# Rotary products on GpSimd in two halves of 128 tokens, and three moves in the instruction orders of GpSimd and ScalarE

## The chip, the cores and the metric

One Trainium2 chip, one core. The time is the device time of one execution in microseconds; three executions were timed, and one more was profiled. A core has a matrix engine (TensorE, PE in the profile), VectorE (DVE), ScalarE (ACT), GpSimd (POOL) and SyncE (SP), whose queue issues nearly all transfers here. Each engine works through its own instruction list in order, and they meet only in semaphores.

## The reference

One layer of a vision transformer on 32 images of 3x224x224: patch embedding, causal attention with rotary positions, and a feed-forward part with fake quantisation. The change lies in the rotary part.

```
h = patches(x) @ W.T + b                     # 32 images x 256 tokens x 256
a = layernorm(h)
q = rope((a @ wq) as 16 heads x 16)          # rope: [t1*cos - t2*sin, t1*sin + t2*cos]
k = rope((a @ wk) as 4 heads x 16); v = a @ wv
attn = softmax(causal(q k^T / 4)); h = h + (attn v) @ wo
f = fake_quant(layernorm(h))                 # one scale over the whole tensor
h = h + fake_quant(silu(f @ Wg.T) * (f @ Wu.T)) @ Wd.T    # weights quantised by row
```

## The kernel before, in words

The first part of the kernel is a software pipeline over images, one step for each. The second part is the feed-forward part, which begins when all images have passed, because its scale is a maximum over all of them. The change touches the first part alone.

In step x each engine runs a list written out by hand, the function `step` in its block, over several images at once. PE embeds image x+3 (`patch`), projects x+2 to q, k and v (`project`, token block tb = 0 or 1 of 128 tokens each), makes the scores of x+1 from which a bound of each row's maximum is taken (`unit_pair`, six of them, "units"), the scores of x-1 and x proper (`score_pair`, eight of them, all in one pair of PSUM banks), the product with the values (`attend`, two halves), the transposes of the result (`o_turn`) and the output projection of x-2 (`out_project`). ScalarE takes the exponential of each score pair (`exp_pair`, L829), takes q, k, v out of PSUM (`projected`, L791, one for each token block), copies v (`values`, L798), writes the high half-precision parts of q and k into two stacks (`high`, L807 and L809, for the units; `fill_stack`, L820 to L822, for the scores), converts the next input (`x_high`, L781) and the attention result (`on_high`, L844), takes out the attention product (`o_copy`, L837) and the embedding (`embedded`, L767 and L772). GpSimd multiplies and adds for the rotation (`rotate_cross` L997, `rotate` L986, `add_rotated` L1011), clears the triangle of each exponential (`mask`, L978), and makes the low part of the input (`x_low`, L1017) and two small powers (L1024). VectorE reduces the units (`reduce_pair`, L1205), writes low parts (`low`, L1191 and L1193; `h_low`, L1211; `on_low`, L1270), normalises the attention product (`o_normalise`, L1252), adds the residual (`residual`, L1262) and does the statistics. SP turns the stacks by DMA transposes in a fixed order in each step: the normalised embedding (L380), the attention result (`turn_on`, L410), the unit stack (`turn_max`, L388), the score stack (`turn_stack`, L400).

The links that the text below follows: `score_pair` i waits for the exponential i-1, since it writes the same banks. `attend` half 0 waits for mask 3, half 1 for mask 7. The rotation waits for `projected`; `high` and `fill_stack` wait for the sum `qk`; `low` waits for `fill_stack`. `on_high` waits for `o_normalise`, `on_low` for `on_high`, `turn_on` for `on_low`, `out_project` for `turn_on`, `residual` for `out_project`. The instructions of VectorE stand in this order: reduce 0, reduce 1, reduce 2, `h_low`, reduce 3, `o_normalise`, reduce 4, `on_low`, reduce 5, `low`, `residual`, and then reduce 0 of the next step, with small statistics between. A unit waits for the reduce of the unit before it.

Of the kernel before, what the change touches and what calls it, by code (L numbers as in the profile page):

```python
# [103 lines left out]
def wait(eng, sem, value):  # L104

    if isinstance(value, int) and value <= 0:
        return
    eng.wait_ge(sem, value)
# [12 lines left out]
def vit_layer(nc, x_t, w_emb, w_qkv, w_o, w_gate, w_up, w_down, clips, rope, eye, tri, out):  # L121
    with ExitStack() as ctx:
# [639 lines left out]
        def _(act):  # L762
# [20 lines left out]
            def projected(x, tb):  # L783
                z = x + 2
                act.wait_ge(done["qkv"], z.n * 2 + (tb + 1))
                if tb == 0:
                    act.wait_ge(rstd_ready, z.n + 1)
                    wait(act, rot_a_ready, z.n)
                    wait(act, rot_b_ready, z.n)
                    wait(act, v_ready, z.n)  # L790
                act.activation(qkv[:, tb, :], shared[JOBS.index(("qkv", tb)) % 2][:, 0:QKV_COLS],  # L791
                               ACT.Copy, scale=rstd[:, tb:tb + 1]).then_inc(read["qkv"], 1)
# [9 lines left out]
            def high(x):  # L802

                z = x + 2
                act.wait_ge(qk_ready, z.n + 1)
                wait(act, max_turned[z.parity - 1], (z + -1).half * 16 + 16)
                act.activation(max_stack[:, :, 0:HEADS, 0:16], qk[:, :, 0:HEADS, :], ACT.Copy, scale=MAX_SCALE)  # L807
                for odd in range(2):
                    op = act.activation(max_stack[:, :, HEADS + 5 * odd:HEADS + 3 + 5 * odd:2, 0:16],  # L809
                                        qk[:, :, HEADS + odd:QK:2, :], ACT.Copy, scale=MAX_SCALE)  # L810
                op.then_inc(high_ready, 1)

            def fill_stack(x):

                z = x + 2
                stack = stacks[z.parity]
                act.wait_ge(qk_ready, z.n + 1)
                wait(act, first_turned[z.parity], z.half * 32)
                wait(act, second_turned[z.parity], z.half * 32)
                act.activation(stack[:, :, :, 16:32], qk[:, :, :, :], ACT.Copy)  # L820
                act.activation(stack[:, :, 0:HEADS, 0:16], qk[:, :, 0:HEADS, :], ACT.Copy)
                act.activation(stack[:, :, HEADS:QK, 32:48], qk[:, :, HEADS:QK, :], ACT.Copy).then_inc(stack_filled, 1)  # L822
# [50 lines left out]
            def step(x):  # L873
                early, late = x + 1, x + -1
                if (x + -1).exists():
                    exp_pair(late, 0)
                if (x + -2).exists():
                    o_copy(late + -1, 1)
                if x.exists():
                    values(late)  # L880
                if (x + -1).exists():
                    exp_pair(late, 1)
                if (x + 1).exists():
                    projected(late, 0)
                    projected(late, 1)
                if (x + -1).exists():
                    exp_pair(late, 2)
                    exp_pair(late, 3)
                if (x + 4).exists():
                    x_high(early)  # L890
                if (x + -2).exists():
                    on_high(late)
                if (x + -1).exists():
                    exp_pair(late, 4)
                if (x + 1).exists():
                    high(late)
                if (x + -1).exists():
                    exp_pair(late, 5)
                if (x + 1).exists():
                    fill_stack(late)  # L900
                if (x + 3).exists():
                    embedded(early)
                if (x + -1).exists():
                    exp_pair(late, 6)
                    o_copy(late, 0)
                    exp_pair(late, 7)
                if (x + -3).exists():
                    normalise2(x)
                if x.known and x.n == -2:
                    weights_turned_copy()  # L910
# [61 lines left out]
        def _(pool):  # L972
# [5 lines left out]
                pool.affine_select(out=p, in_=p, pattern=[[0, 4], [1, P]], compare_op=ALU.is_ge,  # L978
                                   fill=0.0, base=0, channel_multiplier=-1).then_inc(masked, 1)

            def rotate(x):

                z = x + 2
                pool.wait_ge(read["qkv"], z.n * 2 + 2)
                wait(pool, qk_ready, z.n)
                pool.tensor_tensor(rot_a, qk_of_qkv, rope_s[:, 0].to_broadcast([P, TB, QK, HD]),  # L986
                                   ALU.mult).then_inc(rot_a_ready, 1)

            def rotate_cross(x):

                z = x + 2
                pool.wait_ge(read["qkv"], z.n * 2 + 2)
                wait(pool, qk_ready, z.n)
                for half in range(2):
                    to = slice(8 * half, 8 * half + 8)
                    of = slice(8 - 8 * half, 16 - 8 * half)
                    op = pool.tensor_tensor(rot_b[:, :, :, to], qk_of_qkv[:, :, :, of],  # L997
                                            rope_s[:, 1, :, :, to].to_broadcast([P, TB, QK, 8]), ALU.mult)
                op.then_inc(rot_b_ready, 1)

            def flat(t):
                return t.rearrange("p b h d -> p (b h d)")

            def add_rotated(x):
                z = x + 2
                wait(pool, high_ready, z.n)
                wait(pool, stack_filled, z.n)
                wait(pool, low_ready, z.n)
                pool.wait_ge(rot_b_ready, z.n + 1)
                pool.wait_ge(rot_a_ready, z.n + 1)  # L1010
                pool.tensor_tensor(flat(qk), flat(rot_a), flat(rot_b), ALU.add).then_inc(qk_ready, 1)  # L1011

            def x_low(v):
                if v.known and v.n == 0:
# [12 lines left out]

            def step(x):
                early, late = x + 1, x + -1
                if (x + -1).exists():  # L1030
                    mask(late, 1)
                if (x + 1).exists():
                    rotate_cross(late)
                    rotate(late)
                    add_rotated(late)
                if (x + -1).exists():
                    mask(late, 2)
                    mask(late, 3)
                    mask(late, 4)
                if (x + 4).exists():  # L1040
                    x_low(early + 3)
                if (x + -1).exists():
                    mask(late, 5)
                    mask(late, 6)
                    mask(late, 7)
                if x.exists():
                    mask(x, 0)
                if (x + 2).exists():
                    power(var_ready, (x + 2).n, rstd, var, rstd_ready, read["qkv"])
                if (x + -2).exists():  # L1050
                    power(var2_ready, (late + -1).n, rstd2s, var2, rstd2_ready, xn2_ready)
# [452 lines left out]
```

## Time and profile before

| | us |
|---|---|
| median of three executions | 823.68 |
| the three | 821.96, 823.68, 827.12 |
| the profiled execution, its time | 827.79 |
| its span from first to last instruction | 826.0 |

| engine | busy us | share of the span |
|---|---|---|
| PE | 669.9 | 81% |
| DVE | 669.2 | 81% |
| ACT | 591.2 | 72% |
| POOL | 571.7 | 69% |

The image pipeline fills most of the span, at about 18 us for a step; the feed-forward part takes the rest. The mean granted TensorE clock is 0.947 of full speed, and 1.00 in the steps that are looked at below. Busy shares are means over all that, so they don't say what a step waits for; for that one step is laid out engine by engine.

### The profile page before, as it was taken

To read this page: it belongs to the slowest core of one execution; us is meant where nothing else is said; L and a number is where in the kernel's file an instruction comes from. 1 tells how busy PE (TensorE), PEld (TensorE's weight loads), DVE (VectorE), ACT (ScalarE), POOL (GpSimd) and SP (SyncE) were. 2 spreads that over 40 slices of the span, in tenths; PEclk is the share of its full clock that TensorE was granted. 3 is DMA by queue.
4 is the path that set the end of the run, shared out by engine and by line. 5 is a ranking of instruction groups with operands and counts; after the bars stand their busy time and mean duration, and the time that the engine had idled before them with its cause. 6 is when DMAs were issued, how large, how long until landed. Compare 5 with 4: busy or idle time off the path is not lost. (4 is left out here: it accounts for less than half of the span.)

```text
span 826.0 us, 20673 instructions
## 1 busy us (share of the span) xinstructions
PE 669.9 (81%) x6706; PEld 384.2 (47%) x6706; DVE 669.2 (81%) x1052; ACT 591.2 (72%) x972; POOL 571.7 (69%) x561
## 2 busy tenths in 40 slices
PE   3577888888888888898888888889766459997894
PEld 2354555454555555555555555555332223332663
DVE  5954889888988898988889889898663359999894
ACT  4345778787788777778877877887665258886783
POOL 0455778787888788888878888886553148884363
PEclk9687999999999999999999999999897769999798
DMA  8235667667566666556656655665443112221499
GB/s 278 58 72 111 129 122 145 144 131 123 127 144 141 134 150 143 126 122 147 144 133 153 140 126 126 144 143 114 92 78 73 50 38 52 51 43 21 68 175 165
DMA packets 245383, 96.56 MB, mean 117 GB/s; under 512 B 222432, under 2 KB 240608, under 8 KB 245344
## 3 DMA queue, kind: packets, MB, share of 16 engines
q1 hardware_dynamic: 236896, 87.69, 48.7%
q0 software_dynamic: 8448, 8.39, 7.0%
q8 instruction: 20, 0.33, 0.2%
q14 instruction: 19, 0.16, 0.1%
HBM read 24.74 MB, written 16.78 MB: 50 GB/s over the span
## 5 line engine op out<-in xcount | busy, mean ns | idle before, releaser
L1205 DVE TENSOR_REDUCE act_all<-pair 128x4 f16<-128x1024 f32 (+1 forms) x192 | 234.4, 1221 | 21.6 <-PE pair L535 20.9
L978 POOL TENSOR_SCALAR_AFFINE_SELECT act_all<-act_all 128x512 f32<-128x512 f32 x128 | 104.5, 827 | 72.5 <-ACT act_all L829 72.5
L829 ACT ACTIVATE ffn<-pair 128x768 f32<-128x768 f32 x128 | 103.2, 806 | 67.3 <-PE pair L552 67.0
L484 PE MATMUL pair<-act_all 128*128 128x256 f16 (+1 forms) x960 | 118.2, 277 | 21.8 <-DVE act_all L1252 18.5
L978 POOL TENSOR_SCALAR_AFFINE_SELECT ffn<-ffn 128x512 f32<-128x512 f32 x128 | 94.0, 736 | 57.8 <-ACT ffn L829 57.0
L829 ACT ACTIVATE act_all<-pair 128x768 f32<-128x768 f32 x128 | 104.1, 813 | 30.7 <-PE pair L552 28.2
L484 PEld LDWEIGHTS pair<-act_all 128*128 128x128 f16 (+1 forms) x960 | 90.8, 99 | 41.5 <-issue 23.3
L1017 POOL TENSOR_TENSOR act_all<-act_all 128x1280 f16<-128x1280 f32 x31 | 81.7, 2636 | 18.3 <-ACT act_all L781 18.3
L550 PE MATMUL pair<-act_all 64*128 64x256 f16 x512 | 73.2, 282 | 18.9 <-DMA act_all<-act_all 10.9
L1191 DVE TENSOR_TENSOR act_all<-act_all 128x512 f16<-128x512 f32 x32 | 40.9, 1279 | 49.1 <-ACT act_all L822 49.1
L498 PE MATMUL pair<-act_all 128*128 128x384 f16 x384 | 76.4, 337 | 0.2 <-ACT act_all L767 0.2
L939 ACT ACTIVATE ffn<-pair,gate_scale 128x512 f32<-128x512 f32 x96 | 60.9, 654 | 15.5 <-PE pair L710 8.0
L591 PE MATMUL pair<-act_all 128*128 128x256 f16 x384 | 51.0, 286 | 17.9 <-DMA act_all<-ffn 17.7
L1270 DVE TENSOR_TENSOR ffn<-act_all,ffn 128x512 f16<-128x512 f32 x32 | 54.4, 1701 | 11.6 <-ACT ffn L844 11.5
L997 POOL TENSOR_TENSOR act_all<-act_all 128x320 f32<-128x320 f32 x64 | 54.5, 871 | 13.3 <-ACT act_all L791 13.3
L837 ACT ACTIVATE act_all<-pair 128x512 f32<-128x512 f32 x64 | 38.0, 593 | 34.0 <-PE pair L570 34.0
L550 PEld LDWEIGHTS pair<-act_all 64*128 64x128 f16 x512 | 25.1, 93 | 76.7 <-issue 36.2
L522 PE MATMUL pair<-act_all 64*128 64x256 f16 x512 | 50.1, 274 | 13.2 <-DVE act_all L1205 12.3
L535 PE MATMUL pair<-act_all,eye_wide 64*128 64x128 bf16 (+1 forms) x768 | 60.5, 236 | 0.0
L1024 POOL TENSOR_TENSOR act_all<-act_all 128x2 f32<-128x2 f32 x64 | 43.9, 701 | 22.4 <-DVE act_all L1290 14.1
L552 PE MATMUL pair<-act_all 64*128 64x128 f16 x512 | 57.5, 220 | 0.0
L1077 POOL TENSOR_TENSOR act_all<-ffn 128x512 f32<-128x512 f32 x32 | 40.8, 1274 | 21.2 <-ACT ffn L927 21.2
(135 smaller groups left out, 1517.8 us busy)
## 6 DMA issues: line engine op xcount, KB each, us to landing
act_all<-x_t SPq DMA_DIRECT2D x32, 640.0 KB, 4.2
out<-act_all SPq DMA_DIRECT2D x32, 256.0 KB, 2.6
out<-ffn POOLq DMA_DIRECT2D x16, 512.0 KB, 6.9
act_all<-act_all SPq DMA_TRANSPOSE x192, 3.0
act_all<-w_down SPq DMA_DIRECT2D x1, 704.0 KB, 8.6
act_all<-w_emb SPq DMA_DIRECT2D x1, 640.0 KB, 4.0
ffn<-w_gate SPq DMA_DIRECT2D x1, 640.0 KB, 7.0
ffn<-w_up SPq DMA_DIRECT2D x1, 640.0 KB, 7.4
```

Source lines behind the costliest of these rows:

```text
L484: mm = pe.matmul(b, xs[0:k, sx, c, tb * P:(tb + 1) * P], we[0:k, sw, c, :], start=(c == 0 and (sx, sw) == PARTS[0]), stop=(c == KC - 1 and ...
L498: mm = pe.matmul(b[:, 0:QKV_COLS], h_t[:, sx, tb, c, :], wqkv[:, sw, c, :], start=(c == 0 and (sx, sw) == PARTS[0]), stop=(c == DC - 1 and ...
L535: mm = pe.matmul(on_diagonal, eye_wide[rows, at_:at_ + P], tri_b[rows, rows].rearrange("p (a t) -> p a t", a=1).to_broadcast([64, n_, 64]) ...
L550: pe.matmul(b[:, 0:TOKENS], op[rows, k, 0:P], op[rows, pair_, :], start=True, stop=True)
L552: mm = pe.matmul(b[:, TOKENS:3 * P], op[rows, k, P:TOKENS], op[rows, pair_, P:TOKENS], start=True, stop=True)
L829: act.activation(probs[i // 4][:, o:o + 2, 0:3, :].rearrange("p h k s -> p h (k s)"), pair[1][:, :].rearrange("p (h c) -> p h c", h=2)[:, ...
L939: act.activation(silu[m % 3][:, 0:cols], bank[2 + m % 3][:, 0:cols], ACT.Silu, scale=gate_scale[:, m:m + 1]).then_inc(silu_ready, 1)
L978: pool.affine_select(out=p, in_=p, pattern=[[0, 4], [1, P]], compare_op=ALU.is_ge, fill=0.0, base=0, channel_multiplier=-1).then_inc(maske ...
L997: op = pool.tensor_tensor(rot_b[:, :, :, to], qk_of_qkv[:, :, :, of], rope_s[:, 1, :, :, to].to_broadcast([P, TB, QK, 8]), ALU.mult)
L1017: pool.tensor_tensor(x_parts[v.parity][:, 1], xt[v.parity], x_parts[v.parity][:, 0], ALU.subtract).then_inc(x_low_ready, 1)
L1205: dve.tensor_reduce(to, pair[2][:, :].rearrange("p (k g t) -> p k g t", k=2, g=n_), AX.X, ALU.max).then_inc(unit_reduced, 1)
L1270: dve.tensor_tensor(on_parts[:, 1], on.rearrange("p b e -> p (b e)"), on_parts[:, 0], ALU.subtract).then_inc(on_low_ready, 1)
```

## The change

GpSimd's rotation is split by token block. `rotate(x, tb)` does the two cross products and then the straight product of one block of 128 tokens, and `add_rotated(x, tb)` its sum; before, each instruction covered both blocks. The first block's products now wait only for that block's `projected`. Both blocks are placed ahead of mask 1 instead of behind it. On ScalarE, `projected` of block 0 moves ahead of exponential 1 (block 1 stays behind it), `high` moves ahead of exponential 4, and `fill_stack` ahead of exponential 5. `high` and `fill_stack` still wait for both blocks. The semaphores' counts follow: two for each image where there was one.

```diff
--- before.py
+++ after.py
@@ -783,10 +783,10 @@
             def projected(x, tb):
                 z = x + 2
                 act.wait_ge(done["qkv"], z.n * 2 + (tb + 1))
+                wait(act, rot_a_ready, z.n * 2 + (tb - 1))
+                wait(act, rot_b_ready, z.n * 2 + (tb - 1))
                 if tb == 0:
                     act.wait_ge(rstd_ready, z.n + 1)
-                    wait(act, rot_a_ready, z.n)
-                    wait(act, rot_b_ready, z.n)
                     wait(act, v_ready, z.n)
                 act.activation(qkv[:, tb, :], shared[JOBS.index(("qkv", tb)) % 2][:, 0:QKV_COLS],
                                ACT.Copy, scale=rstd[:, tb:tb + 1]).then_inc(read["qkv"], 1)
@@ -802,7 +802,7 @@
             def high(x):
 
                 z = x + 2
-                act.wait_ge(qk_ready, z.n + 1)
+                act.wait_ge(qk_ready, z.n * 2 + 2)
                 wait(act, max_turned[z.parity - 1], (z + -1).half * 16 + 16)
                 act.activation(max_stack[:, :, 0:HEADS, 0:16], qk[:, :, 0:HEADS, :], ACT.Copy, scale=MAX_SCALE)
                 for odd in range(2):
@@ -814,7 +814,7 @@
 
                 z = x + 2
                 stack = stacks[z.parity]
-                act.wait_ge(qk_ready, z.n + 1)
+                act.wait_ge(qk_ready, z.n * 2 + 2)
                 wait(act, first_turned[z.parity], z.half * 32)
                 wait(act, second_turned[z.parity], z.half * 32)
                 act.activation(stack[:, :, :, 16:32], qk[:, :, :, :], ACT.Copy)
@@ -878,10 +878,11 @@
                     o_copy(late + -1, 1)
                 if x.exists():
                     values(late)
+                if (x + 1).exists():
+                    projected(late, 0)
                 if (x + -1).exists():
                     exp_pair(late, 1)
                 if (x + 1).exists():
-                    projected(late, 0)
                     projected(late, 1)
                 if (x + -1).exists():
                     exp_pair(late, 2)
@@ -890,14 +891,14 @@
                     x_high(early)
                 if (x + -2).exists():
                     on_high(late)
+                if (x + 1).exists():
+                    high(late)
                 if (x + -1).exists():
                     exp_pair(late, 4)
                 if (x + 1).exists():
-                    high(late)
+                    fill_stack(late)
                 if (x + -1).exists():
                     exp_pair(late, 5)
-                if (x + 1).exists():
-                    fill_stack(late)
                 if (x + 3).exists():
                     embedded(early)
                 if (x + -1).exists():
@@ -978,37 +979,30 @@
                 pool.affine_select(out=p, in_=p, pattern=[[0, 4], [1, P]], compare_op=ALU.is_ge,
                                    fill=0.0, base=0, channel_multiplier=-1).then_inc(masked, 1)
 
-            def rotate(x):
+            def rotate(x, tb):
 
                 z = x + 2
-                pool.wait_ge(read["qkv"], z.n * 2 + 2)
-                wait(pool, qk_ready, z.n)
-                pool.tensor_tensor(rot_a, qk_of_qkv, rope_s[:, 0].to_broadcast([P, TB, QK, HD]),
-                                   ALU.mult).then_inc(rot_a_ready, 1)
-
-            def rotate_cross(x):
-
-                z = x + 2
-                pool.wait_ge(read["qkv"], z.n * 2 + 2)
-                wait(pool, qk_ready, z.n)
+                pool.wait_ge(read["qkv"], z.n * 2 + (tb + 1))
+                wait(pool, qk_ready, z.n * 2 + (tb - 1))
+                at_ = slice(tb, tb + 1)
                 for half in range(2):
                     to = slice(8 * half, 8 * half + 8)
                     of = slice(8 - 8 * half, 16 - 8 * half)
-                    op = pool.tensor_tensor(rot_b[:, :, :, to], qk_of_qkv[:, :, :, of],
-                                            rope_s[:, 1, :, :, to].to_broadcast([P, TB, QK, 8]), ALU.mult)
+                    op = pool.tensor_tensor(rot_b[:, at_, :, to], qk_of_qkv[:, at_, :, of],
+                                            rope_s[:, 1, at_, :, to].to_broadcast([P, 1, QK, 8]), ALU.mult)
                 op.then_inc(rot_b_ready, 1)
-
-            def flat(t):
-                return t.rearrange("p b h d -> p (b h d)")
-
-            def add_rotated(x):
+                pool.tensor_tensor(rot_a[:, at_], qk_of_qkv[:, at_], rope_s[:, 0, at_].to_broadcast([P, 1, QK, HD]),
+                                   ALU.mult).then_inc(rot_a_ready, 1)
+
+            def add_rotated(x, tb):
                 z = x + 2
                 wait(pool, high_ready, z.n)
                 wait(pool, stack_filled, z.n)
                 wait(pool, low_ready, z.n)
-                pool.wait_ge(rot_b_ready, z.n + 1)
-                pool.wait_ge(rot_a_ready, z.n + 1)
-                pool.tensor_tensor(flat(qk), flat(rot_a), flat(rot_b), ALU.add).then_inc(qk_ready, 1)
+                pool.wait_ge(rot_b_ready, z.n * 2 + (tb + 1))
+                pool.wait_ge(rot_a_ready, z.n * 2 + (tb + 1))
+                pool.tensor_tensor(qk[:, tb].rearrange("p h d -> p (h d)"), rot_a[:, tb].rearrange("p h d -> p (h d)"),
+                                   rot_b[:, tb].rearrange("p h d -> p (h d)"), ALU.add).then_inc(qk_ready, 1)
 
             def x_low(v):
                 if v.known and v.n == 0:
@@ -1027,13 +1021,12 @@
 
             def step(x):
                 early, late = x + 1, x + -1
+                if (x + 1).exists():
+                    for tb in range(TB):
+                        rotate(late, tb)
+                        add_rotated(late, tb)
                 if (x + -1).exists():
                     mask(late, 1)
-                if (x + 1).exists():
-                    rotate_cross(late)
-                    rotate(late)
-                    add_rotated(late)
-                if (x + -1).exists():
                     mask(late, 2)
                     mask(late, 3)
                     mask(late, 4)
```

## Rows read from the trace of the kernel before

**Rows 1.** Windows of one step: length, busy us and count of each engine, granted clock.
```profile
301.30:319.54 18.24, 15.99 (x183) 9.70 (x184) 16.26 (x27) 14.53 (x26) 15.00 (x16) 1.00 0.62 137
500.00:518.00 18.00, 15.80 (x183) 9.58 (x184) 16.00 (x27) 14.40 (x26) 14.90 (x16) 1.00 0.61 139
```
**Rows 2.** Timeline of DVE: start, us, line, operation, idle before and releaser.
```profile
309.56 0.68 DVE L1211 TENSOR_TENSOR act_all<-act_all 128x512 f16<-128x512 f16 x1
311.83 0.69 DVE L1252 TENSOR_TENSOR act_all<-pair,act_all 128x512 f32<-128x512 f32 x1
314.07 2.05 DVE L1270 TENSOR_TENSOR ffn<-act_all,ffn 128x512 f16<-128x512 f32 x1 [0.40 <-ACT ffn L844]
...
319.54 1.39 DVE L1191 TENSOR_TENSOR act_all<-act_all 128x512 f16<-128x512 f32 x1 [1.32 <-ACT act_all L822]
...
321.49 0.68 DVE L1262 SCALAR_TENSOR_TENSOR act_all<-pair,act_all 128x512 f32<-128x512 f32 x1
322.09 1.21 DVE L1205 TENSOR_REDUCE act_all<-pair 128x8 f16<-128x1024 f32 x1
```
**Rows 3.** Timeline of PE in the same step.
```profile
305.55 0.39 PE L516 MATMUL pair<-act_all 64*128 64x128 f16 x8
...
306.09 1.07 PE L566 MATMUL pair<-ffn 128*32 128x512 f32 x8
...
309.53 0.28 PE L550 MATMUL pair<-act_all 64*128 64x256 f16 x2
...
312.77 1.80 PE L484 MATMUL pair<-act_all 128*128 128x256 f16 x15 [0.72 <-DVE act_all L1252]
...
316.85 0.28 PE L550 MATMUL pair<-act_all 64*128 64x256 f16 x2
```
**Rows 4.** Timeline of ACT in the same step.
```profile
307.65 0.60 ACT L837 ACTIVATE act_all<-pair 128x512 f32<-128x512 f32 x1 [1.00 <-PE pair L570]
308.14 0.30 ACT L798 ACTIVATE ffn<-act_all 128x128 f32<-128x128 f32 x1
308.56 0.81 ACT L829 ACTIVATE act_all<-pair 128x768 f32<-128x768 f32 x1
309.27 1.05 ACT L791 ACTIVATE act_all<-pair,act_all 128x384 f32<-128x384 f32 x2
...
313.42 0.62 ACT L844 ACTIVATE ffn<-act_all 128x512 f16<-128x512 f32 x1
...
315.69 0.63 ACT L807 ACTIVATE act_all<-act_all 128x512 f16<-128x512 f32 x1
...
317.23 0.81 ACT L829 ACTIVATE ffn<-pair 128x768 f32<-128x768 f32 x1 [0.61 <-PE pair L552]
317.94 0.73 ACT L820 ACTIVATE act_all<-act_all 128x640 f16<-128x640 f32 x1
```
**Rows 5.** Timeline of POOL in the same step.
```profile
309.54 1.21 POOL L978 TENSOR_SCALAR_AFFINE_SELECT act_all<-act_all 128x512 f32<-128x512 f32 x1 [0.76 <-ACT act_all L829]
310.72 1.67 POOL L997 TENSOR_TENSOR act_all<-act_all 128x320 f32<-128x320 f32 x2
312.34 1.55 POOL L986 TENSOR_TENSOR act_all<-act_all 128x640 f32<-128x640 f32 x1
314.03 1.54 POOL L1011 TENSOR_TENSOR act_all<-act_all 128x640 f32<-128x640 f32 x1
...
317.15 0.63 POOL L978 TENSOR_SCALAR_AFFINE_SELECT ffn<-ffn 128x512 f32<-128x512 f32 x1
317.76 2.63 POOL L1017 TENSOR_TENSOR act_all<-act_all 128x1280 f16<-128x1280 f32 x1
```
**Rows 6.** Timeline of DVE in another step.
```profile
404.43 0.69 DVE L1270 TENSOR_TENSOR ffn<-act_all,ffn 128x512 f16<-128x512 f32 x1 [0.40 <-ACT ffn L844]
```
**Rows 7.** Timeline of POOL in that step.
```profile
404.43 2.09 POOL L1011 TENSOR_TENSOR act_all<-act_all 128x640 f32<-128x640 f32 x1 [0.17 <-POOL act_all L986]
```
**Rows 8.** Timeline of SP in the first step: start, time of issue.
```profile
316.14 1.23 SPq L410 DMA_TRANSPOSE act_all<-ffn  x1
```

## The prediction

> **What bounds the kernel now.** I read first the windows, one step of the image pipeline each: a step takes 18.24 us in one place and 18.00 in another, at full granted clock in both, and in the first DVE is busy 16.26, PE 15.99, POOL 15.00 and ACT 14.53 [rows 1]. No engine is full. So a step is held by a loop of waits that comes round once per image, and the timelines of the engines are laid side by side to find it. The reader is to look for bracketed idle times, and for starts that follow hard on another engine's end.
>
> The loop: DVE starts `low` at 319.54 after 1.32 idle, released by the last write of `fill_stack` [rows 2]. From there DVE hardly pauses: residual, reduces 0 to 3 and `o_normalise`, which ends at 311.83 + 0.69 = 312.52 one step earlier. PE has waited 0.72 for it and starts `patch` at 312.77, then runs through to score pair 5 at 316.85 [rows 3]. ACT has waited 0.61 for that, takes exponential 5 at 317.23 and only then writes the stack, from 317.94 [rows 4]. That frees `low` at 319.54. It is 18.24 long, a whole step. The change takes exponential 5 out of it.
>
> A second loop runs close beside it: score pair 2 at 309.53 [rows 3], then score pair 3, exponential 3, `x_high`, `on_high` at 313.42 [rows 4], `on_low` at 314.07 [rows 2], `turn_on` at 316.14 [rows 8], the transposes queued behind it, and the next step's score pairs. DVE waits 0.40 for `on_high` in it.
>
> **Who holds up whom between DVE and POOL.** `on_low` takes 2.05 us in the first step, with POOL's `add_rotated` beginning 0.04 ahead of it (314.03) and lasting 1.54 [rows 2, 5]. In another step both begin at 404.43; DVE's takes 0.69 and POOL's 2.09, that is 0.55 more than its 1.54 [rows 6, 7]. So one excludes the other for a whole instruction, and the loser is delayed by the winner. Likewise mask 1, begun together with `h_low`, takes 1.21 for 0.63 [rows 2, 5]: 0.57 for each such meeting. And `low`, begun at 319.54 under `x_low` (317.76 to 320.39), ends at 320.93, which is 0.54 after `x_low`'s end.
>
> The Trainium skill states this lock in "SBUF — State Buffer", section "Who interferes with whom": a DVE instruction with two SBUF inputs and a GpSimd instruction that reads SBUF exclude each other, and whichever starts first keeps the pair for its whole length. The trace agrees, with the 2.05 and 0.69 above. By it smaller instructions on POOL shorten DVE's waits, which speaks for the change, and an earlier `low` gains nothing while `x_low` runs, which speaks against it.
>
> **The change part by part.**
>
> Rotation. Removed: two cross products of 320 elements (start to start 1.62 / 2 = 0.81 each), one product of 640 (1.55) and one sum of 640 (1.54), together 4.85 from 310.72 to the sum's end at 315.57 [rows 5]. Added: four cross products of 160 elements, two products and two sums of 320. The 320 takes 0.81 from start to start; the 640 takes 1.50 (its 1.55 less the 0.05 by which successive rows overlap). No row shows 160 elements. By the straight line through 320 and 640, 160 costs 0.81 - 0.69/2 = 0.465. The nearest row alone bounds it below at 0.41 (half of 0.81). Above, I take the slope from 640 to 1280 elements, (2.63 - 1.54)/640 = 1.70 ns each, which leaves 0.81 - 0.27 = 0.54 by distance from 320, or 0.68 if the fixed part is what this slope leaves of the 640 row (1.50 - 1.09 = 0.41, and 0.27). I take 0.465, since it lies between the nearest two sizes of the same operation. Sum: 4 x 0.465 + 4 x 0.81 = 5.10. Between a block's product and its sum POOL waits for its own result: the gap from 312.34 + 1.55 to 314.03 is 0.14; once before, twice now: 0.3. `h_low` now falls into the rotation instead of onto mask 1, and `on_low`, at a time when shorter instructions run, gets in between two of them: 0.57 each, 1.14. With 0.05 for the end of the last row, the rotation takes R = 5.10 + 0.3 + 1.14 + 0.05 = 6.6 us, where it took 4.85.
>
> Its start. `projected` 0 moves from 309.27 to right behind `values` (308.14) [rows 4]: start 308.36, end 308.94, rotation from 309.1, 1.6 earlier than 310.72. Its end: 309.1 + 6.6 = 315.7, against 315.57. So the halves and the early start buy nothing at the place where `qk` is whole.
>
> `projected` 0 ahead of exponential 1 delays that one by about 0.3 (308.56 to 308.84), and with it score pair 2, which now starts at 309.8 for 309.53 [rows 3, 4]. The second loop grows by it.
>
> `high` ahead of exponential 4. `on_high` is done at 313.42 + 0.62 = 314.04 [rows 4]; `high` can start at 315.8. ACT stands still in between, some 1.7 us, a new wait, and behind it are queued exponential 4 and all that follows. `high` took from 315.69 to 316.62 (exponential 5's start less its idle time), 0.93; exponential 4 therefore ends at about 317.5 to 317.7, where before it was over when `high` began at 315.69. Score pair 5 (316.85 before), mask 4 and `x_low` wait for that. On SP, `turn_max` waits for `high`, which would be done at 316.7, and stands behind `turn_on`, whose issue lasts to 316.14 + 1.23 = 317.37 [rows 8]: no new wait in that queue.
>
> `fill_stack` ahead of exponential 5. It ends about 0.3 sooner than before and would take 1.3 us of DVE's wait away; but `x_low` has begun by then (it starts 0.8 after exponential 4's end, `fill_stack` ends 1.3 after it), so `low` waits for the lock instead of for the stack. Late next is `x_low`.
>
> Masks 1 to 3 behind the rotation: before, mask 1 stood ahead of it and masks 2 and 3 behind. `attend` 0 needs mask 3; with the three at 0.63 it starts at about 317.9 for 317.34, still behind the delayed score pair 5, so it costs nothing more.
>
> **The new loop.** From reduce 0's start: 1.21 its length, 0.1 to PE (estimated from the 0.25 after `o_normalise`, the longest such step shown), 0.54 for unit 1 (305.55 to 306.09), 1.56 for `attend` 1 (to 307.65), 0.49 `o_copy`, 0.22 `values`, 0.58 `projected` 0, 0.16 to POOL (exponential 1's end at 309.37 to 309.54): 4.9 [rows 3 to 5]. Then R = 6.6. Then 0.12 to ACT (315.57 to 315.69), 0.93 `high`, 0.81 exponential 4, 0.16 to POOL, 0.63 mask 4, 2.63 `x_low`, and from its end to the next reduce 0 322.09 - 320.39 = 1.70 with `low` and `residual` in it [rows 2, 4, 5]: 7.0. Sum 18.45 us for a step, against a mean of 18.12 [rows 1]: 0.33 more. The loop through the second stack and `out_project` is shorter by about 0.6 and doesn't decide.
>
> Of 32 images I count 28 steps that run at the full overlap. 28 x 0.33 = +9.2 us. On the profiled execution's 827.79 (span 826.0 and 1.8 around it) that is 837.0. The median of the runs shown is 0.995 of the profiled time: 832.8, 1.1% slower. The feed-forward part is untouched: 0.
>
> At this place a page would change the number. The Trainium skill, "Perfetto Trace Analysis", section "GPSIMD Engine Instruction", says that a GpSimd instruction's reported span is unreliable and that spacing from start to start is to be used. I did so. By the reported 0.86 and 1.55 instead, the sum would be some 0.4 longer a step, and the time 844; the trace's own rows overlap by 0.05, so the spacing is right as far as they show.
>
> **The rivals.**
>
> Faster. If the rotation ends before `on_high` does, ACT doesn't stand still and the second loop decides: from score pair 2 at 309.53 to `on_low` at 314.07 4.54; `on_low` 0.69 instead of 2.05 since its opponent is short [rows 2, 6], with up to 0.5 of waiting; from its old end 316.12 to the next step's score pair 2, 309.53 + 18.24, 11.65; exponential 1's delay 0.3. That is 17.2 to 17.7. Midway, 0.6 less a step, gives 28 x 0.6 = 17 us: 807. It needs R below about 5.7, so both meetings with DVE avoided; for it speaks that the order in which the two engines ask is a matter of 0.1 us (the 0.04 above). A partial case, at 17.8 a step, is 815. Chance 0.2 for these.
>
> No change. The estimate by half of 320 (0.41, and 0.75 for the rest) gives R = 6.1 and a step of 17.95; one meeting avoided gives the same. Or `low` asks ahead of `x_low`. Within 1% of before means within 0.29 us a step, which is also about the least a measurement of this kernel can tell from nothing. 820 to 831. Chance 0.33.
>
> Much slower. If a small POOL operation has the fixed part that the 640 and 1280 rows would leave, 160 costs 0.68: R grows by 4 x 0.215 = 0.9, a step to 19.3, and 28 x 1.2 = 34 us: 857. The line through three shapes of one size class speaks against it. Chance 0.07.
>
> My forecast, slower by 0.5% to 2.5% (828 to 845), has 0.4; a piece of it lies within 1%.
>
> **How the numbers follow.** Slower by over 1%: most of the forecast's 0.4 and the 0.07, 0.44. Within 1%: 0.34 with the forecast's lower edge. Faster by over 1%: 0.22. The range goes from the partial faster case (815, less a little for the lead-in: 812) to the forecast's upper edge with one more 0.2 a step (850).
>
> **What would show it.** ACT idle ahead of L807, released by POOL's sum, over 1 us a step, where it was nearly 0. Rotation products of 0.5 and 0.85 us, with one longer by 0.57 beside L1211. L1191 at over 2 us with the idle time before it gone. L1270 near 1 us instead of 2. The exponential 4 and `x_low` later against `o_normalise` by 1 us or more. The forecast is wrong if ACT's wait before L807 stays under 0.5 us, or if a 160 element product takes 0.4 or less, or if `low` comes ahead of `x_low` in POOL's order of time.

## The result and the profile after

| | before | after |
|---|---|---|
| median of 13 executions, us | 823.72 | 829.05 |
| lowest and highest | 820.75, 827.30 | 827.30, 831.54 |
| ratio to before, 95% interval | | 1.0059 [1.0042, 1.0075] |

The changed kernel is 0.6% slower, clear of the noise; the forecast was 1.1% slower. The profiled executions happen to lie at opposite ends of the two spreads (827.79 before, 827.30 after; spans 826.0 and 825.6), so the two traces are compared step by step and not by their spans. The first line is the page's: engine, busy us, share, instructions.

```profile
PE 666.7 (81%) x6706; PEld 381.5 (46%) x6706; DVE 663.3 (80%) x1052; ACT 586.9 (71%) x972; POOL 591.5 (72%) x689
```

POOL has 128 instructions and 20 us more. For the step, first POOL's timeline, which answers to [rows 5].

```profile
305.99 1.44 POOL L991 TENSOR_TENSOR act_all<-act_all 128x160 f32<-128x160 f32 x2 [0.62 <-ACT act_all L791]
307.39 0.86 POOL L994 TENSOR_TENSOR act_all<-act_all 128x320 f32<-128x320 f32 x1
308.42 0.86 POOL L1004 TENSOR_TENSOR act_all<-act_all 128x320 f32<-128x320 f32 x1 [0.17 <-POOL act_all L994]
309.24 1.00 POOL L991 TENSOR_TENSOR act_all<-act_all 128x160 f32<-128x160 f32 x2
310.20 0.86 POOL L994 TENSOR_TENSOR act_all<-act_all 128x320 f32<-128x320 f32 x1
311.24 1.28 POOL L1004 TENSOR_TENSOR act_all<-act_all 128x320 f32<-128x320 f32 x1 [0.17 <-POOL act_all L994]
312.48 1.80 POOL L979 TENSOR_SCALAR_AFFINE_SELECT act_all<-act_all 128x512 f32<-128x512 f32 x3
314.43 0.63 POOL L979 TENSOR_SCALAR_AFFINE_SELECT ffn<-ffn 128x512 f32<-128x512 f32 x1
315.03 2.63 POOL L1011 TENSOR_TENSOR act_all<-act_all 128x1280 f16<-128x1280 f32 x1
```

The rotation lasts from 305.99 to its last sum's end at 312.52, 6.53 us, where it took 4.85. Two undisturbed cross products take 1.00; the first pair takes 1.44, and the last sum 1.28 instead of 0.86. DVE's timeline shows who was in the way, and answers to [rows 2].

```profile
306.22 0.83 DVE L1204 TENSOR_TENSOR act_all<-act_all 128x512 f16<-128x512 f16 x1
...
311.11 0.69 DVE L1263 TENSOR_TENSOR ffn<-act_all,ffn 128x512 f16<-128x512 f32 x1 [0.40 <-ACT ffn L844]
...
315.77 2.44 DVE L1184 TENSOR_TENSOR act_all<-act_all 128x512 f16<-128x512 f32 x1 [1.32 <-ACT act_all L822]
...
319.36 1.21 DVE L1198 TENSOR_REDUCE act_all<-pair 128x8 f16<-128x1024 f32 x1
...
334.06 2.45 DVE L1184 TENSOR_TENSOR act_all<-act_all 128x512 f16<-128x512 f32 x1 [1.22 <-ACT act_all L822]
```

`h_low` (L1204) falls into the first cross products and `on_low` (L1263) comes just ahead of the last sum; it takes 0.69 where it took 2.05. `low` (L1184) takes 2.44 where it took 1.39: it begins at 315.77, 0.74 after `x_low` has begun (315.03), and ends at 318.21, 0.55 after `x_low`'s end (before, it ended 0.54 after it too). ACT answers to [rows 4].

```profile
305.25 0.58 ACT L791 ACTIVATE act_all<-pair,act_all 128x384 f32<-128x384 f32 x1
305.73 0.80 ACT L829 ACTIVATE act_all<-pair 128x768 f32<-128x768 f32 x1
...
310.46 0.62 ACT L844 ACTIVATE ffn<-act_all 128x512 f16<-128x512 f32 x1
312.64 0.63 ACT L807 ACTIVATE act_all<-act_all 128x512 f16<-128x512 f32 x1 [1.57 <-POOL act_all L1004]
...
313.47 0.79 ACT L829 ACTIVATE ffn<-pair 128x768 f32<-128x768 f32 x1
```

ACT stands 1.57 us ahead of `high`, released by POOL's sum. The groups of L807 from 230 to 560 us, first of before and then of after (busy, mean ns, idle before), show the same over 18 steps, with 27.4 / 18 = 1.52 us on the mean:

```profile
L807 ACT ACTIVATE act_all<-act_all 128x512 f16<-128x512 f32 x18 | 11.3, 629 | 1.0 <-POOL act_all L1011 1.0
```

```profile
L807 ACT ACTIVATE act_all<-act_all 128x512 f16<-128x512 f32 x18 | 11.3, 630 | 27.4 <-POOL act_all L1004 27.4
```

PE answers to [rows 3]: it now waits for exponential 1 ahead of score pair 2 and for exponential 4 ahead of score pair 5.

```profile
306.59 0.28 PE L550 MATMUL pair<-act_all 64*128 64x256 f16 x2 [0.33 <-ACT act_all L829]
...
314.32 0.28 PE L550 MATMUL pair<-act_all 64*128 64x256 f16 x2 [0.36 <-ACT ffn L829]
```

How far do the steps account for the time? I measure a step from the end of one `low` to the end of the next. Between the eleventh `low` and the 29th, 18 steps, its median is 18.09 us before; after, it goes to and fro between 18.30 and 18.38 (297.38 to 315.77 and to 334.06 in the starts), median 18.34. That is 0.25 more. But not every step is like these. Between the fifth and the eleventh the kernel before has two long steps, of 19.29 and 19.70, and the changed one only one of 18.74, so from the fifth `low` to the last the change costs 3.7 us and not 28 times 0.25. The lead-in gives some back: the fifth `low` ends at 118.61 before and at 116.01 after, 2.6 sooner, of which 1.9 are in the step from the first `low` to the second (16.42 and 14.55). Behind the last `low`, where the change does nothing, the trace of before is 1.5 longer, at a mean granted clock of 0.88 against 0.90. The two traces together thus differ by 0.4 us and with the other sign than the medians, 823.7 and 829.05: they are single executions, 4.1 above and 1.8 below their kernels' medians. The step's growth and the lead-in add up to 1 to 2 us more for the changed kernel; where the rest of the 4.9 us (0.0059 of 823.7) lies, these two traces don't show.

### The profile page after: what moved, and what is told of

It is laid out like the page before. It is cut to its first block and busy times, and to the rows that moved or that the text cites. A ratio compares the mean times of both kernels' runs of the same rounds, so it can differ in the third digit from the quotient of the medians.

```text
span 825.6 us, 20928 instructions
## 1 busy us (share of the span) xinstructions
PE 666.7 (81%) x6706; PEld 381.5 (46%) x6706; DVE 663.3 (80%) x1052; ACT 586.9 (71%) x972; POOL 591.5 (72%) x689
## 5 line engine op out<-in xcount | busy, mean ns | idle before, releaser
L979 POOL TENSOR_SCALAR_AFFINE_SELECT act_all<-act_all 128x512 f32<-128x512 f32 x128 | 78.4, 633 | 43.2 <-ACT act_all L829 43.2
L1184 DVE TENSOR_TENSOR act_all<-act_all 128x512 f16<-128x512 f32 x32 | 69.8, 2181 | 41.2 <-ACT act_all L822 41.2
L991 POOL TENSOR_TENSOR act_all<-act_all 128x160 f32<-128x160 f32 x128 | 76.4, 618 | 27.2 <-ACT act_all L791 27.2
L1004 POOL TENSOR_TENSOR act_all<-act_all 128x320 f32<-128x320 f32 x64 | 68.1, 1064 | 10.8 <-POOL act_all L994 10.5
L807 ACT ACTIVATE act_all<-act_all 128x512 f16<-128x512 f32 x32 | 20.2, 630 | 53.2 <-POOL act_all L1004 53.2
```

What stands on the lines that cost most here:

```text
L991: op = pool.tensor_tensor(rot_b[:, at_, :, to], qk_of_qkv[:, at_, :, of], rope_s[:, 1, at_, :, to].to_broadcast([P, 1, QK, 8]), ALU.mult)
L1004: pool.tensor_tensor(qk[:, tb].rearrange("p h d -> p (h d)"), rot_a[:, tb].rearrange("p h d -> p (h d)"), rot_b[:, tb].rearrange("p h d -> ...
L1184: dve.tensor_tensor(stack[:, :, 0:HEADS, 32:48], qk[:, :, 0:HEADS, :], stack[:, :, 0:HEADS, 16:32], ALU.subtract)
```

## The experiments

"Step" is always the median of the 18 steps between the ends of the eleventh and the 29th `low` in that run's trace, as above: 18.09 before, 18.34 after. Each ratio is to executions of the kernel before that were taken beside the run; their medians are 825.17 for experiments 1 to 4, 824.78 for 5 to 8, and 825.82 for 9 to 11. Times of different experiments are therefore compared by their ratios.

**1. The halves alone**, behind mask 1, with ScalarE's order of before.

```diff
# POOL, against after; ACT's list is that of before
-                    for tb in range(TB):
-                        rotate(late, tb)
-                        add_rotated(late, tb)
                     mask(late, 1)
+                    for tb in range(TB):
+                        rotate(late, tb)
+                        add_rotated(late, tb)
```

> The rotation by blocks alone, still behind mask 1, with ScalarE's order as before. Theory of the loop through GpSimd: the rotation takes about 1 us longer (six instructions become eight, a second wait of 0.17), its sum and with it x_low come about 1 us later, and low, which waits for x_low's end, too; the old loop had about 0.3 to 0.5 us to spare against that, so 0.1 to 0.5 us a step more: 827 to 838. Theory that splitting is free and the orders alone cost: within 2 us of before.

Measured 836.74, ratio 1.0145 [1.0124, 1.0167], step 18.56: slower than the whole change. (It is four instructions that become eight; the expectation miscounts them, its 1 us doesn't rest on that.) POOL's timeline, then DVE's:

```profile
314.60 1.31 POOL L993 TENSOR_TENSOR act_all<-act_all 128x320 f32<-128x320 f32 x1
316.08 0.86 POOL L1003 TENSOR_TENSOR act_all<-act_all 128x320 f32<-128x320 f32 x1 [0.17 <-POOL act_all L993]
...
318.67 2.62 POOL L1010 TENSOR_TENSOR act_all<-act_all 128x1280 f16<-128x1280 f32 x1
```

```profile
320.18 1.66 DVE L1184 TENSOR_TENSOR act_all<-act_all 128x512 f16<-128x512 f32 x1 [2.65 <-ACT act_all L822]
```

The rotation (from 310.84) is whole at 316.9, 6.1 us after its start against 4.85, and `low` waits 2.65 for the stack and then for `x_low`'s end (321.29; it ends 0.55 later). ACT stands ahead of `high` here too, 1.24 us in this step, with its order of before. Splitting is not free, and of the parts tried by themselves it is the dearest.

**2. ScalarE's two moves alone.**

```diff
# ACT, against before
+                    high(late)
                     exp_pair(late, 4)
-                    high(late)
+                    fill_stack(late)
                     exp_pair(late, 5)
-                    fill_stack(late)
```

> Only ScalarE's two moves (high ahead of exponential 4, fill_stack ahead of exponential 5), with the whole rotation behind mask 1. Theory of the loop: ScalarE stands still some 1.6 us ahead of high, exponential 4 and mask 4 come that much later, x_low starts later, low waits for it; a step of about 18.3, as after: 826 to 832. Rival, that the early projected 0 (which delays exponential 1) is what costs: the order alone is free or gains what DVE waited for the stack, 806 to 823.

Measured 831.90, ratio 1.0082 [1.0060, 1.0104], step 18.22, with some of 18.7. ACT's row, and DVE's:

```profile
315.00 0.63 ACT L807 ACTIVATE act_all<-act_all 128x512 f16<-128x512 f32 x1 [1.52 <-POOL act_all L1011]
```

```profile
318.12 2.43 DVE L1191 TENSOR_TENSOR act_all<-act_all 128x512 f16<-128x512 f32 x1 [0.59 <-ACT act_all L822]
```

The same stand of ScalarE and the same `low` under `x_low`, without any split and with exponential 1 in its old place. The rival is refuted: the order by itself costs, in the kernel before.

**3. The two moves taken back out of the change.** The diff is the reverse of experiment 2, against after.

> The change with high and fill_stack put back behind exponentials 4 and 5. Theory of the loop: mask 4 is held by masks 1 to 3 behind the rotation as much as by exponential 4 (0.15 us between them in the trace), so x_low moves up by only 0.15 us a step: 823 to 828. Rival, that the 1.5 us stand of ScalarE is itself the price: most of a us a step comes back, below 815.

Measured 828.29, ratio 1.0034 [1.0016, 1.0053], step 18.21, just above the upper edge of what the loop gave. ACT no longer waits for POOL, and yet:

```profile
311.88 1.81 POOL L979 TENSOR_SCALAR_AFFINE_SELECT act_all<-act_all 128x512 f32<-128x512 f32 x3
313.64 0.63 POOL L979 TENSOR_SCALAR_AFFINE_SELECT ffn<-ffn 128x512 f32<-128x512 f32 x1
314.24 2.62 POOL L1011 TENSOR_TENSOR act_all<-act_all 128x1280 f16<-128x1280 f32 x1
```

From the start of mask 1 to `x_low` it is 2.36 us here and 2.55 in the change: the four masks are in the way either way. The 1.57 us stand is worth 0.13 us a step by the traces, and 0.07 by the ratios.

**4. `x_low` ahead of mask 4**, in the changed kernel.

```diff
# POOL, against after
                     mask(late, 3)
+                    x_low(early + 3)
                     mask(late, 4)
-                    x_low(early + 3)
                     mask(late, 5)
```

> The change with x_low placed ahead of mask 4 instead of behind it. Theory of the loop: x_low starts 0.75 us earlier (at mask 3's end, not after exponential 4 and mask 4), low gets the shared port that much earlier, until unit 0 and the DMA queue hold reduce 0: a step of 17.7 instead of 18.34, 810 to 816 us. Rival, that the halves' extra instructions or exponential 1's delay hold the step: no change, 827 to 831.

Measured 819.68, ratio 0.9943 [0.9926, 0.9959], step 17.97. POOL's row, and DVE's:

```profile
311.54 2.64 POOL L1011 TENSOR_TENSOR act_all<-act_all 128x1280 f16<-128x1280 f32 x1
```

```profile
313.04 1.68 DVE L1184 TENSOR_TENSOR act_all<-act_all 128x512 f16<-128x512 f32 x1 [1.32 <-ACT act_all L822]
...
315.64 0.69 DVE L1255 SCALAR_TENSOR_TENSOR act_all<-pair,act_all 128x512 f32<-128x512 f32 x1 [0.28 <-issue]
```

The time is between the two expectations. `low` is 0.76 shorter, as the lock asks, and the step 0.37 shorter, not 0.6: DVE now idles 0.28 ahead of the residual, which needs `out_project`, and that stands behind score pair 6 and exponential 5 (PE waits 0.28 for it), behind `fill_stack`.

**5. The same move in the kernel before.** The diff is that of experiment 4.

> The kernel before with x_low ahead of mask 4. Theory: there low asks for the port at 319.54 and would get it some 0.6 us sooner, but reduce 0 is held by unit 0 and out_project, which were only 0.06 us ahead of it; a step shorter by 0 to 0.1: 820 to 825. Rival, that x_low's place by itself is worth what it gave in the changed kernel: 815 to 818.

Measured 820.11, ratio 0.9938 [0.9907, 0.9969], step 17.90. The time is inside what was expected, but the step is 0.2 shorter, twice the bound; the 0.06 was only the last of the waits of the second loop, and the others had more to give. So `x_low` is a part of before's loop too, and its place is worth about half there of what it is worth in the change (5.1 us against 9.6 by the ratios).

**6. Projected 0 back behind exponential 1**, in the changed kernel.

```diff
# ACT, against after
-                    projected(late, 0)
                     exp_pair(late, 1)
+                    projected(late, 0)
                     projected(late, 1)
```

> The change with projected 0 put back behind exponential 1. Theory of the loop: exponential 1 (0.7 us) and the wait for it come back into the loop ahead of the rotation, a step of 19.1 to 19.3, 845 to 858 us. Rival, that exponential 1's delay by projected 0 is what costs in the change: faster than the change, back to 824 or less.

Measured 833.74, ratio 1.0096 [1.0062, 1.0129], step 18.48. The rival is refuted, since it got slower, but the size missed by far: 0.14 a step, not 0.9. POOL's timeline says why.

```profile
308.88 1.11 POOL L990 TENSOR_TENSOR act_all<-act_all 128x160 f32<-128x160 f32 x2 [1.28 <-ACT act_all L791]
...
313.80 1.10 POOL L1003 TENSOR_TENSOR act_all<-act_all 128x320 f32<-128x320 f32 x1 [0.17 <-POOL act_all L993]
314.85 1.81 POOL L978 TENSOR_SCALAR_AFFINE_SELECT act_all<-act_all 128x512 f32<-128x512 f32 x3
```

Measured from the start of `o_copy`, `projected` 0 and with it the rotation start 0.67 later (306.58 to 308.14 here, 304.36 to 305.25 in the change), and the rotation takes 6.01 instead of 6.53, because `h_low` is nearly over when it starts and `on_low` costs its last sum less. The early start buys 0.67 us and pays 0.52 of it back in the shared port; the 0.15 that is left is what the step shows.

**7. One more product of 320 elements a step** on POOL.

```diff
# POOL, rotate(x, tb), against after, ahead of the straight product
+                if tb == 0:
+                    wait(pool, spare_done, z.n)
+                    pool.tensor_tensor(spare..., qk_of_qkv[:, 0], rope_s[:, 0, 0]..., ALU.mult).then_inc(spare_done, 1)
```

> The change with one more product of 320 elements a step on GpSimd, into a spare tile, ahead of block 0's straight product. Theory of the loop: the rotation lies whole on the path that sets the step, so a step grows by the product's full 0.81 us, to 19.15: 850 to 854. Rival, that GpSimd has slack and PE or the DMA queue hold the step: under 0.3 us a step, at most 837.

Measured 851.34, ratio 1.0307 [1.0273, 1.0340], step 18.98. By the ratios 20.4 us more, 0.73 for each of 28 steps, and 0.64 by the step, out of the product's 0.82: the rotation lies on the path that sets the step. POOL as a whole idles over 2 us a step all the while. What is missing of the 0.82 shows in POOL's last sum and DVE's `on_low`:

```profile
322.47 1.09 POOL L1009 TENSOR_TENSOR act_all<-act_all 128x320 f32<-128x320 f32 x1 [0.17 <-POOL act_all L999]
```

```profile
321.52 1.33 DVE L1268 TENSOR_TENSOR ffn<-act_all,ffn 128x512 f16<-128x512 f32 x1 [0.40 <-ACT ffn L846]
```

POOL's last product (321.44) is now under way when `on_low` comes, so `on_low` is the one that is held longer, and the sum is held less, 1.09 where it took 1.28 in the change.

**8. `x_low` early and the two moves taken back**, the diffs of 4 and 3 together.

> The change with x_low ahead of mask 4, and with high and fill_stack back behind exponentials 4 and 5. With x_low out of the way, PE's waits for exponentials 4 and 5 (0.36 and 0.28 us a step, both behind the stacks on ScalarE) and through them out_project and the residual hold reduce 0; without them a step of 17.5 to 17.8 where xlow_early has 17.97: 808 to 816. Rival, that the second loop through on_low and the DMA queue holds it already: the same as xlow_early, 818 to 821.

Measured 814.26, ratio 0.9862 [0.9835, 0.9889], step 17.67: faster than both kernels, by 1.4% than before. The rival is refuted. DVE's row:

```profile
313.46 0.86 DVE L1184 TENSOR_TENSOR act_all<-act_all 128x512 f16<-128x512 f32 x1 [2.13 <-ACT act_all L822]
```

`low` waits for the stack again, 2.13 us, and hardly for the port.

**9. `h_low` ahead of reduce 2**, in the changed kernel.

```diff
# DVE, against after
+                    h_low(early)
                     reduce_pair(x, 2)
-                    h_low(early)
```

> The change with VectorE's h_low ahead of reduce 2 instead of behind it, so that it asks for the shared port before the rotation begins. Theory of the loop, in which each meeting between a VectorE subtraction and a rotation instruction lengthens the rotation: the first cross products take 1.0 instead of 1.44 us for the pair, the rotation 6.1 instead of 6.5, and a step 0.2 to 0.4 less: 817 to 824. Rival: reduce 2 comes 0.6 us later and with it unit 3, which has only 0.4 us to spare, and the meeting isn't on the path: 829 or more.

Measured 816.65, ratio 0.9897 [0.9864, 0.9930], step 17.80: 0.54 less, a little beyond what was expected. POOL's timeline, DVE's rows, ACT's row:

```profile
301.55 1.00 POOL L991 TENSOR_TENSOR act_all<-act_all 128x160 f32<-128x160 f32 x2 [0.59 <-ACT act_all L791]
...
306.35 0.86 POOL L1004 TENSOR_TENSOR act_all<-act_all 128x320 f32<-128x320 f32 x1 [0.17 <-POOL act_all L994]
307.16 2.27 POOL L979 TENSOR_SCALAR_AFFINE_SELECT act_all<-act_all 128x512 f32<-128x512 f32 x3
```

```profile
300.66 0.68 DVE L1204 TENSOR_TENSOR act_all<-act_all 128x512 f16<-128x512 f16 x1
...
310.45 2.71 DVE L1184 TENSOR_TENSOR act_all<-act_all 128x512 f16<-128x512 f32 x1 [0.22 <-ACT act_all L822]
```

```profile
307.33 0.63 ACT L807 ACTIVATE act_all<-act_all 128x512 f16<-128x512 f32 x1 [0.47 <-POOL act_all L1004]
```

`h_low` is over at 301.34, before the rotation begins. The rotation takes 5.66 instead of 6.53: both meetings are gone from it. One of them has only moved: `on_low` now meets a mask, the three masks take 2.27 for 1.80, and from the start of mask 1 to `x_low` it is 2.83 (`x_low` starts at 309.99) for 2.55. So the step gains 0.54 and not the whole 0.87. ACT's stand shrinks from 1.57 to 0.47, and `low` still ends 0.55 after `x_low`. Two instructions exchanged on VectorE turn the change from 0.6% slower to 1.0% faster than before.

**10. Both ideas together**, `h_low` early in the kernel of experiment 8.

> The fastest version so far (x_low ahead of mask 4, high and fill_stack back behind their exponentials) with h_low ahead of reduce 2. Here low waits 2.13 us for fill_stack and no longer for x_low, so a shorter rotation lies beside other work: within 3 us of 814. Rival, that the rotation holds the step there too: 806 to 810.

Measured 825.91, ratio 0.9999 [0.9971, 1.0027], step 17.95, going from 17.8 to 18.4, 18.05 on the mean: 11 us slower than experiment 8 by the ratios. Both expectations missed. `low` still waits 2.13 us for the stack, and DVE stands 0.60 ahead of reduce 3 for PE, as in experiment 9; with reduce 2 later by `h_low`'s 0.6, unit 3 and score pair 3 come later. That this is the path there, by way of score pairs, exponential 5 and `fill_stack`, is argued from these waits and was not tried by itself. The trace shows a second candidate, on POOL:

```profile
307.18 1.86 POOL L1018 TENSOR_TENSOR act_all<-act_all 128x2 f32<-128x2 f32 x2
309.01 0.99 POOL L991 TENSOR_TENSOR act_all<-act_all 128x160 f32<-128x160 f32 x2
```

Here `h_low` (307.82 to 308.49) meets the second of the two small powers. That one takes 1.19 instead of 0.69, in every other step, and the rotation waits behind it: it begins 1.19 after `h_low`'s start in those steps, and 0.63 after it in the others. So the early place of `h_low` doesn't avoid POOL here; it meets another instruction of it.

**11. Projected 0 back** in the kernel of experiment 8.

> The same fastest version with projected 0 back behind exponential 1. In the changed kernel that cost 0.65 us ahead of the rotation and gave 0.53 back by missing h_low. Where the rotation is no longer on the path, it should cost nothing or give up to 0.3 us a step, since exponential 1 and score pair 2 (0.36 us of PE's wait) come sooner: 806 to 815. Rival, that the early rotation carries the gain: 818 to 822.

Measured 819.11, ratio 0.9915 [0.9889, 0.9941], step 17.87: inside the rival's range and outside the loop's, 0.2 a step slower than experiment 8, somewhat more than experiment 6 showed. So the early `projected` 0 is a gain there too; whether the early rotation is what gains, or something else that follows `projected` 0, stays open.

## Why the prediction was right, and where its sizes were off

**The loop.** The path was right: ACT stands ahead of `high`, exponential 4 comes later, and `low` runs into `x_low`'s hold on the shared port. Forecast 18.45 us a step, measured 18.34. In the step shown, against the prediction's sum: from reduce 0 (300.98) to the rotation 5.0 (forecast 4.9), the rotation 6.53 (6.6), to `x_low` 2.5 (2.65), `x_low` 2.6 (2.63), to the next reduce 0 1.7 (1.70). The same path in the step of before takes 6.85, 4.85, 2.19, 2.6 and 1.7. So the change gains 1.8 by the early start, loses 1.7 by the longer rotation and 0.3 between rotation and `x_low`. Experiments 2, 4, 7 and 9 each touch one link and move the time the way that the loop says; experiment 9 takes the meetings out of the rotation.

The outcome with the largest chance, slower by over 1% (0.44), did not come. The 0.6% is the lower edge of the forecast and lies within 1%, which had 0.34. Not every sign came true either. Against `o_normalise`, exponential 4 is later by 1.54 us (from 314.88 to 313.47, where `o_normalise` moved from 311.83 to 308.88), but `x_low` only by 0.22, where the sign asked for 1 or more. And `low` still waits 1.32 for the stack ahead of its 2.44; that idle time was to be gone.

**The rotation.** Forecast 6.6, measured 6.53. A cross product of 160 elements follows the one before it after some 0.48 (0.465 taken), the second inner wait is there (0.17), the two meetings cost 0.44 and 0.42 instead of 0.57 each; `h_low` had begun 0.25 ahead of the second product that it held up, and `on_low` 0.13 ahead of the sum.

**ACT's stand** was given as some 1.7 and is 1.57, 1.52 on the mean. Score pair 5 waits 0.36. `on_low` takes 0.69; I had "near 1".

**The terms that were mis-sized.** The growth of a step was forecast as 0.33 and is 0.25: the old step was taken as 18.12 and is 18.09, the new one was 0.11 too long. It was multiplied by 28, but only some 18 steps grew like that; over all steps behind the fifth `low` it came to 3.7 us in the traces, where the sum had 9.2. The gain in the lead-in was left out. It is 2.6 us in these traces, and its largest part, 1.9 in the second `low`'s step, belongs to the split: that step takes 14.48 to 15.06 in nine of the ten kernels with halves (16.06 in experiment 10's), and 16.42 to 17.02 in the three without. By the two traces loop and lead-in thus make 1 to 2 us, by the medians the change costs 4.9, and the forecast was 9.2. The distance to the forecast has its causes in these terms, but how much each weighs in the medians the two traces can't tell. Within the loop, the stand's price was not what the prediction's order of telling suggests: without it the masks hold `x_low` nearly as long (experiment 3, some 0.1 a step). Putting mask 1 behind the rotation, GpSimd's own move, and the early start without the halves were never tried by themselves, so their shares in the result are not shown. And exponential 1's delay, counted as a cost to the second loop, cost nothing that can be seen, as the sum had it; the move that causes it is a gain (experiment 6).

**The other loops.** For experiment 5 I read 0.06 us of room from the last wait ahead of reduce 0. It gave 0.2 a step. The loop through `out_project`, which the prediction put 0.6 shorter, shows in experiment 4, at 0.37 less. The waits further up the loop have to be added up, not the last one taken.

**The faster rival** did not come in the change itself, but its condition could be made with one exchange of instructions: it asked for R below about 5.7, "both meetings with DVE avoided", and experiment 9 has R of 5.66 with both out of the rotation, at 816.65 where that rival's partial case had 815. Its mechanism came in part: ACT still stands 0.47 ahead of `high`.

The lock itself was taken from two rows and from the Trainium skill ("SBUF — State Buffer", section "Who interferes with whom"). It held in the rows of every run shown here: the instruction that began second was delayed, by up to 2.0 us (`low` in experiment 9, 2.71 against 0.69). Where two starts lie within some 0.04 us the trace doesn't tell who goes first: mask 1 begins 0.02 ahead of `h_low` and is the one that is delayed [rows 2, 5]. Much of the change's price is set by who is second.

## What to carry to other kernels

Cutting an operation in two pays only if a consumer takes the first half early; here `high` and `fill_stack` still wait for both, so the halves brought four more instructions, one more round trip and a meeting, 1.25 us in experiment 1, and no consumer that starts sooner. (A kernel with such a consumer was not tried.) Ahead of moving an operation on GpSimd, lay VectorE's subtractions of two tiles in SBUF beside it: a meeting costs both ways, and changing the order of two neighbours on VectorE gained 1.6% in the changed kernel, more than the whole change had cost. It is no rule, though: in the kernel of experiment 8 the same exchange cost 1.4%, so look again after each other change. An engine's wait that a trace shows (1.57 us) is not what its removal gives: here that was some 0.1 a step, since the next link was 0.14 behind (mask 4's wait for exponential 4).

## What the runs showed of the hardware

A VectorE subtraction of 128x512 with both inputs in SBUF took 0.69 us alone, 2.44 when begun 0.74 after a GpSimd operation of 2.63, and 2.71 when begun 0.46 after it: it ended 0.55 after that one's end, in each step. Even a GpSimd operation on two elements a partition was held up by such a subtraction, 1.19 for 0.69 (experiment 10). GpSimd's products took 0.52 for 160 elements, 0.86 for 320 and 1.55 for 640, which is one straight line with a fixed part of some 0.17. By experiment 9 the cut costs 5.66 - 4.85 = 0.81 us a step without any meeting: 0.17 for one more round trip, and 0.64 for four more instructions, 0.16 each. The two meetings of the change added 0.87. The changed kernel's steps repeat to 0.1 us over some twenty steps, where the kernel before scatters from 17.8 to 18.4: that several loops of almost one length take turns there is likely, and was not followed step by step.
